# A gram product of 128 rows split into two of 64 rows, in two PSUM banks, in a three-layer CIN on one core

## The chip, the core and the metric

One core of one Trainium2 chip. The metric is the device time of one execution in microseconds (us); of several runs the median is taken. A difference of under 0.2% is about what a measurement of this kernel can't tell from no change.

## What is computed

A compressed interaction network over 512 samples, 39 fields of 16 dimensions each, three layers of 128 outputs, and a small dense tower behind it:

```python
def _cin_layer(X0, Xi, W, b):
    H = W.shape[0]
    F0_, Fi = (X0.shape[1], Xi.shape[1])
    Wr = W.reshape(H, F0_, Fi)
    return jnp.einsum('hjk,bjd,bkd->bhd', Wr, X0, Xi) + b[None, :, None]
X0 = embedded_features                 # 512 x 39 x 16, gathered from 39 tables
Xi = X0
for W, b in Ws:                        # 3 layers
    Xi = _cin_layer(X0, Xi, W, b)
    res.append(Xi.sum(axis=2))
h = concat(res, dense_ctx); y = relu(relu(h @ W_top1 + b1) @ W_top2 + b2) @ W_top3
```

Only the sum over the 16 dimensions of the third layer is wanted. So the kernel forms, for each sample, the product of the second layer's output with X0 summed over the dimensions (the *gram*: 128 outputs by 39 fields and one column of plain sums), and multiplies by the third layer's weights once at the end.

## The kernel before, in words

The batch is cut into 16 groups of 32 samples (`GROUPS`), each of 4 tiles (`TILES`) of 8 samples. A tile has 8 samples times 16 dimensions, so 128 rows, one per partition; rows 0 to 63 belong to its first four samples. T counts the 64 tiles through all groups, t is the tile in its group.

Each engine runs its own program and they meet through semaphores. In a tile the following is done:

- **TensorE** (PE) makes the second layer in ten *banks*, `layer1_bank` (L1111): bank m holds four fields (bank 9 three) times 128 outputs, by three products (L1124, L1125, L1128) of high and low halves. Before a bank it waits until the PSUM bank that it writes is free (`bank_free`, L1104). Banks 1, 2, 4, 5, 7, 8 and 9 go through a ring of four PSUM banks, banks 0, 3 and 6 through a ring of two. After bank 3 (`GRAM_AT`) stands the gram of the tile two back (`gram_product(T - 2, t % 2)`, L1096, its matmul L1101): the 128 rows of `x2` against `bdiag`, 8 samples times 40 columns, 320 columns into one PSUM bank, `pq`. It waits for `x2_ready`, `bdiag_ready` and the copy of the gram before. At seven slots of a group (`LAYER0_SLOTS`), one of them after bank 4 of tile 0, a piece of the next group's first layer stands (L1089 and, for two pieces, L1076 to L1086).
- **ScalarE** (ACT) scales the seven banks field by field, in place (L765). After bank 4 of tile 3 it also takes the next group's first layer out of PSUM (`high_part`, L733); after bank 4 of each tile it copies the gram two back from `pq` to SBUF (L737).
- **VectorE** (DVE) scales banks 0 and 3 into an accumulator of 9 columns per output (L914, counted by `dve_scaled`) and bank 6 in place (L919), adds the other banks to the accumulator (L935), and folds the accumulator into `x2` (L941), which sets `x2_ready`. In `low_part` (L896) it makes the low half of the next group's input.
- **GpSimd** (POOL) writes `bdiag` (`spread`, L544) for the tile: X0 times a mask, so that a row meets only its own sample's 40 columns. It waits for the gram of the tile two back, which read the same buffer. It also gathers the embeddings by indirect DMA (L497) and makes the first layer's pairs (L568).

The order on DVE is written out by hand. "sum before" and "fold before" belong to the tile in front:

```python
DVE_ORDER = (("sum before", 8), ("scale", 0), ("sum before", 9), ("scale", 3), ("sum", 1), ("sum", 2),
             ("sum", 4), ("fold before", 0), ("scale", 6), ("sum", 5), ("sum", 7), ("sum", 6))
SEAM_ORDER = tuple(x for x in DVE_ORDER if x[0] != "fold before") + (("fold before", 0),)
```

`SEAM_ORDER` holds for tile 3 of a group: the low half goes behind "sum 4" and the fold of tile 2 to the very end. The gram that reads this fold stands after bank 3 of tile 0 of the next group. There are 15 such seams. The groups 2 to 13 run in a loop of two, the others are written out. The program and its semaphores are otherwise the same in all tiles.

Of the kernel before, what the change touches and what calls it, by code (L numbers as in the profile page):

```python
# [5 lines left out]
F32 = mybir.dt.float32  # L6
F32R = mybir.dt.float32r
I32 = mybir.dt.int32
ALU = mybir.AluOpType
# [3 lines left out]
P = 128  # L13
BATCH, FIELDS, DIM, HID = 512, 39, 16, 128
# [5 lines left out]
TILE_B = P // DIM  # L20
# [4 lines left out]
NT = GROUPS * TILES  # L25
# [17 lines left out]
BANKS = -(-FIELDS // BANK_F)  # L43
LAST_F = FIELDS - BANK_F * (BANKS - 1)
GRAM = FIELDS + 1

ACT_BANKS = (1, 2, 4, 5, 7, 8, 9)  # L50
DVE_BANKS = (0, 3, 6)
N_ACT, N_DVE = len(ACT_BANKS), len(DVE_BANKS)
ACT_RING, DVE_RING = 4, 2
RING = ACT_RING + DVE_RING
N_ACC = 2
BEGINS = DVE_BANKS[0:N_ACC]
PARTS = N_ACC * BANK_F + 1


DVE_ORDER = (("sum before", 8), ("scale", 0), ("sum before", 9), ("scale", 3), ("sum", 1), ("sum", 2),  # L60
             ("sum", 4), ("fold before", 0), ("scale", 6), ("sum", 5), ("sum", 7), ("sum", 6))
SEAM_ORDER = tuple(x for x in DVE_ORDER if x[0] != "fold before") + (("fold before", 0),)
SUM_ORDER = (1, 2, 4, 5, 7, 6, 8, 9)
# [55 lines left out]
def tower(nc, dense_ctx, ids, table, bases, W_top1, b_top1, W_top2, b_top2, W_top3,  # L119
          W0, b0, W1, b1, W2, b2, out):  # L120
    ctx = ExitStack()
    with ctx:
        def sb(name, shape, dt=F32):
            return ctx.enter_context(nc.sbuf_tensor(name, shape, dt))

        def pb(name):
            return ctx.enter_context(nc.psum_tensor(name, [P, 512], F32))

        def sem(name):
            return ctx.enter_context(nc.semaphore(name))  # L130


        ident = sb("ident", [P, P])
        mask = sb("mask", [P, TILE_B])
        ids_all = sb("ids_all", [P, GROUPS, PER_Q], I32)
        base = sb("base", [P, PER_Q], I32)
        idx = [sb(f"idx{u}", [P, PER_Q], I32) for u in range(2)]
# [3 lines left out]
        x0t = [sb(f"x0t{u}", [P, TILES, COLS]) for u in range(2)]  # L141
# [10 lines left out]
        b1c = sb("b1c", [P, HID])  # L152
        acc = [sb(f"acc{u}", [P, HID, PARTS]) for u in range(2)]
        x2 = [sb(f"x2_{u}", [P, HID]) for u in range(2)]
        bdiag = [sb(f"bdiag{u}", [P, TILE_B, GRAM]) for u in range(2)]
        spare = [sb(f"spare{i}", [P, BATCH], F32R) for i in range(8)]
        ctx_wide = sb("ctx_wide", [P, TOP1], F32R)
        ctx_tall = sb("ctx_tall", [P, BATCH], F32R)
        gram = sb("gram", [P, GRAM, BATCH])
        z0 = sb("z0", [P, BATCH])  # L160
# [43 lines left out]
        x0d = nc.dram_tensor("x0_scratch", [2, ROWS_D, GROUP_N], F32, kind="Internal").ap()  # L204


        yb = [pb(f"yb{i}") for i in range(RING)]
        ya, yd = yb[0:ACT_RING], yb[ACT_RING:RING]
        p0 = pb("p0")
        pq = pb("pq")  # L210


        ids_in = sem("ids_in")
# [15 lines left out]
        consts = sem("consts")  # L229
# [28 lines left out]
        dve_scaled = sem("dve_scaled")  # L258
# [3 lines left out]
        gram_done = sem("gram_done")  # L262
        gram_copied = sem("gram_copied")
# [27 lines left out]
        def y_bank(t, m):  # L291

            if m in ACT_BANKS:
                return ya[(t * N_ACT + ACT_BANKS.index(m)) % ACT_RING]
            return yd[(t * N_DVE + DVE_BANKS.index(m)) % DVE_RING]

        def sums_by(T, m):

# [14 lines left out]
        def at_least(T, n):  # L313

            return not isinstance(T, int) or T >= n
# [41 lines left out]
        def _(sp):  # L357
# [101 lines left out]
            load_rolled(1, 1)  # L459
            period(0, 0)  # L460
            stack_weights()
            sp.wait_ge(consts, 10)
            for at in CTX_AT:
                sp.dma_start(dctx[:, :, at:at + CTX], dense_ctx.rearrange("(c p) n -> p c n", p=P)).then_inc(ctx_in, 16)
            period(1, 1)
# [18 lines left out]
        def _(pool):  # L484
# [10 lines left out]
            def gather(u, i):  # L495
# [3 lines left out]


            pool.memset(ident[:, :], 1.0).then_inc(consts, 1)
            pool.memset(mask[:, :], 1.0).then_inc(consts, 1)
            pool.wait_ge(consts, 1)
            pool.affine_select(out=ident[:, :], in_=ident[:, :], compare_op=ALU.is_equal, fill=0.0,
                               base=0, pattern=[[-1, P]], channel_multiplier=1).then_inc(consts, 1)
            pool.wait_ge(consts, 3)
            pool.affine_select(out=mask[:, :], in_=mask[:, :], compare_op=ALU.is_ge, fill=0.0,
                               base=0, pattern=[[-DIM, TILE_B]], channel_multiplier=1).then_inc(consts, 1)
            pool.wait_ge(consts, 4)
            pool.affine_select(out=mask[:, :], in_=mask[:, :], compare_op=ALU.is_ge, fill=0.0,  # L510
                               base=DIM - 1, pattern=[[DIM, TILE_B]], channel_multiplier=-1).then_inc(consts, 1)
            pool.wait_ge(consts, 5)
            for u in range(2):
                pool.tensor_copy(bdiag[u][:, :, FIELDS], mask[:, :]).then_inc(consts, 1)
            for u in range(2):
                pool.memset(emb[u][:, :, :], 0.0).then_inc(consts, 1)
            pool.memset(dctx[:, :, :], 0.0).then_inc(consts, 1)
            pool.wait_ge(consts, 9)
            pool.wait_ge(ids_in, 16 * 2)
            for u in range(2):  # L520
                if u == 1:
# [15 lines left out]
            def spread(g, t, u):  # L537
                T = g * TILES + t

                if t == 0:  # L540
                    pool.wait_ge(x0t_in[u], (g + 2 - u) * (8 * TILES))
                if at_least(T, 2):
                    pool.wait_ge(gram_done, T - 1)
                pool.tensor_tensor(bdiag[t % 2][:, :, 0:FIELDS],  # L544
                                   mask[:, :, None].to_broadcast([P, TILE_B, FIELDS]),
                                   x0t[u][:, t, None, 0:FIELDS].to_broadcast([P, TILE_B, FIELDS]),
                                   ALU.mult).then_inc(bdiag_ready, 1)

            def sum_dims(g, u):
# [122 lines left out]
        def _(act):  # L672
# [7 lines left out]
            def copy_weights(n):  # L680

                act.wait_ge(w_turned, n + 1)
                if n < W0_BANKS:
                    for i in range(4 * n, min(4 * n + 4, CHUNKS)):
                        rows = ROWS if i < CHUNKS - 1 else LAST_ROWS
                        op = act.activation(w0t[0:rows, i, :], yb[n % RING][0:rows, (i % 4) * HID:(i % 4 + 1) * HID], ACT.Copy)
                    op.then_inc(w_hi, 1)
                else:
                    j = 4 * (n - W0_BANKS)
                    w = min(4, FIELDS - j) * HID  # L690
                    act.activation(w1h[:, j * HID:j * HID + w], yb[n % RING][:, 0:w], ACT.Copy).then_inc(w_hi, 1)

# [42 lines left out]
            def copy_gram(T):  # L735
                act.wait_ge(gram_done, T + 1)
                act.activation(gram[:, :, bass.ds(T * TILE_B, TILE_B)],  # L737
                               pq[:, 0:TILE_B * GRAM].rearrange("p (b c) -> p c b", c=GRAM),
                               ACT.Copy).then_inc(gram_copied, 1)

            def high_weights():
# [123 lines left out]
        def _(dve):  # L865
# [17 lines left out]
            def low_weights(n):  # L883
# [3 lines left out]
                if n >= W0_BANKS + W_BANKS:  # L887
                    dve.tensor_copy(w2flat[:, j * HID:j * HID + w], yb[n % RING][:, 0:w]).then_inc(w_lo, 1)
                    return
                dve.wait_ge(w_hi, n + 1)  # L890
                dve.tensor_tensor(w1l[:, j * HID:j * HID + w], yb[n % RING][:, 0:w],
                                  w1h[:, j * HID:j * HID + w].bitcast(F32), ALU.subtract).then_inc(w_lo, 1)
# [103 lines left out]

        @block.tensor
        def _(pe):
            pe.wait_ge(consts, 9)
            pe.wait_ge(w0_sym, 2 * HALF + 1)  # L1000

            def wait_bank(n):
# [90 lines left out]
                if c == CHUNKS - 1:  # L1093
                    op.then_inc(l0_done, 1)

            def gram_product(T, p):  # L1096
                pe.wait_ge(x2_ready, T + 1)
                pe.wait_ge(bdiag_ready, T + 1)
                if at_least(T, 1):
                    pe.wait_ge(gram_copied, T)  # L1100
                pe.matmul(pq[:, 0:TILE_B * GRAM], x2[p][:, :], bdiag[p][:, :, :].rearrange("p b c -> p (b c)"),  # L1101
                          start=True, stop=True).then_inc(gram_done, 1)

            def bank_free(T, m):  # L1104

                if m in BEGINS:
                    pe.wait_ge(dve_scaled, T * N_DVE + BEGINS.index(m) + 1)
                else:
                    pe.wait_ge(summed, sums_by(T, m))

            def layer1_bank(g, t, u, m, low=None):  # L1111
                T = g * TILES + t
                of, ring = (ACT_BANKS, ACT_RING) if m in ACT_BANKS else (DVE_BANKS, DVE_RING)
                k = of.index(m)
                if k >= ring:
                    bank_free(T, of[k - ring])
                elif at_least(T, 1):
                    bank_free(T - 1, of[k - ring])
                y = y_bank(t, m)
                w = fields_of(m) * HID  # L1120
                at = BANK_F * m * HID
                cols = slice(t * P, (t + 1) * P)
                hi, lo = x1h[u][:, cols], x1l[u][:, cols]
                pe.matmul(y[:, 0:w], hi, w1h[:, at:at + w], start=True, stop=False)  # L1124
                pe.matmul(y[:, 0:w], hi, w1l[:, at:at + w], start=False, stop=False)  # L1125
                if low is not None:
                    pe.wait_ge(x1l_ready, low)
                pe.matmul(y[:, 0:w], lo, w1h[:, at:at + w], start=False,  # L1128
                          stop=True).then_inc(bank_ready, 1)
# [42 lines left out]
                period(it * 2 + 1, 1, 2)  # L1172
            period(GROUPS - 2, 0, 1)
            period(GROUPS - 1, 1, 0)
            gram_product(NT - 2, 0)

            def layer2_plain(h):

# [18 lines left out]
            pe.wait_ge(dense_split, 8)  # L1197
            pe.wait_ge(summed, NT * N_SUM)
            first_terms(0)
            gram_product(NT - 1, 1)  # L1200
            for c in range(1, TOP1 // P):
                first_terms(c)
            pe.wait_ge(gram_copied, NT)
# [1 line left out]
            for i in range(FIELDS - PLAIN):  # L1205
# [8 lines left out]
                op = pe.matmul(p0[:, :], w2h[:, w], gram_l[r], start=False, stop=(j == FIELDS - 1))  # L1214
# [16 lines left out]
            for c in range(TOP1 // P):  # L1231
                pe.matmul(yb[c][:, :], wt1h[2][:, c * P:(c + 1) * P], zl[2], start=False,
                          stop=True).then_inc(h1_done, 1)
            for c in range(TOP1 // P):
                pe.wait_ge(h1_ready, c + 1)
                for o in range(TOP2 // P):
                    op = pe.matmul(yd[o][:, :], wt2[:, c, o * P:(o + 1) * P], h1[c],  # L1237
                                   start=(c == 0), stop=(c == TOP1 // P - 1))
                    if c == TOP1 // P - 1:
                        op.then_inc(h2_done, 1)  # L1240
            for c in range(TOP2 // P):
                pe.wait_ge(h2_ready, c + 1)
                op = pe.matmul(p0[0:1, :], wt3[:, c:c + 1], h2[c], start=(c == 0), stop=(c == TOP2 // P - 1))
# [39 lines left out]
```

## Time and profile before

| what | value |
|---|---|
| median of 3 runs | 657.04 us |
| lowest and highest run | 656.72 and 657.56 us |
| span of the profiled execution, first to last instruction | 664.5 us |
| TensorE clock granted, mean over the span | 0.995 of full (1.0 is 2.4 GHz) |
| PE, DVE, ACT, POOL busy, share of the span | 95%, 85%, 84%, 67% |

The profiled execution is one of its own, and its span is the only time that the page gives of it. Its span is 7.5 us over the median of the runs that were timed without a profile. Times in rows are counted from its first instruction. The ends of matmuls are modelled: a matmul's row is longer than its share of the array, and the distance from the start of one to the start of the next tells what it costs. "x2" with the gram is its two weight loads and two passes, which the trace shows as two matmuls.

### The profile page before, as it was taken

How to read it: one execution, taken by the hardware profiler on the slowest of the kernel's cores; microseconds unless marked ns; L12 is line 12 of the kernel's file. 1: busy time of each engine (PE TensorE's matmuls, PEld its weight loads, DVE VectorE, ACT ScalarE, POOL GpSimd, SP SyncE). 2: the span in 40 equal slices, each digit the busy share in tenths (PEclk: the TensorE clock that was granted, in tenths of full speed). 3: DMA queues.
4: the chain of work that ended last, by engine and by line, in shares of the span. 5: the costliest groups of instructions: out<-in, count | busy, mean ns of one | idle time of the engine just before them, and what ended most of it. 6: DMA issues, size and time to landing. Idle time of an engine off the chain costs nothing.

```text
span 664.5 us, 11375 instructions
## 1 busy us (share of the span) xinstructions
PE 633.7 (95%) x2616; PEld 477.0 (72%) x2616; DVE 561.9 (85%) x878; ACT 557.3 (84%) x1940; POOL 443.1 (67%) x504
## 2 busy tenths in 40 slices
PE   2689999999999999999999999999999999989998
PEld 2656767777777777777777777777777777767874
DVE  3538788889899898989898989898989989899890
ACT  2348788989898999999998999998989998999773
POOL 7555897777777778687777787777777535152700
PEclk9799999999999999999999999999999999999999
DMA  8245533242424233242423333323242320200000
GB/s 292 22 61 105 162 38 87 51 87 56 84 56 80 59 58 84 40 102 33 90 41 84 57 86 55 87 52 81 57 85 55 67 68 6 69 27 0 1 0 1
DMA packets 91117, 43.58 MB, mean 66 GB/s; under 512 B 80630, under 2 KB 83780, under 8 KB 88943
## 3 DMA queue, kind: packets, MB, share of 16 engines
q1 hardware_dynamic: 84058, 41.77, 28.1%
q0 software_dynamic: 5120, 1.29, 2.2%
q10 hardware_dynamic: 1904, 0.15, 0.2%
q14 instruction: 25, 0.20, 0.1%
q8 instruction: 10, 0.16, 0.1%
HBM read 36.39 MB, written 1.81 MB: 57 GB/s over the span
## 4 chain that ended last, share of the span: by engine, by line
PE 75%; DVE 8%; ACT 7%; issue 6%; DMA 3%; DVEq 1%; POOL 0%; SPq 0%; another core or an unknown queue 0%
PE yb L1128 16%; PE yb L1124 16%; PE yb L1125 16%; PE p L1089 10%; PE pq L1101 6%; ACT yb L765 5%; DVE x L941 3%; DVE acc L935 3%; DMA gram<-in_L_rec_W_dram 2%; PE yb L1026 2%; DMA emb<-in_table_dram,idx 1%; DVE x1l L896 1%; PE yb L1237 1%; PE p L1182 1%; PE p L1214 1%
## 5 line engine op out<-in xcount | busy, mean ns | idle before, releaser
L765 ACT ACTIVATE yb<-yb,x0t 128x128 f32<-128x128 f32 x1728 | 467.2, 391 | 56.0 <-PE yb L1128 49.6
L935 DVE TENSOR_TENSOR acc<-acc,yb 128x512 f32<-128x512 f32 (+1 forms) x512 | 323.4, 674 | 33.8 <-ACT yb L765 30.9
L1124 PE MATMUL yb<-w1h,x1h 128*128 128x512 f32 (+1 forms) x640 | 293.8, 459 | 5.0 <-DVE acc L935 3.8
L1128 PE MATMUL yb<-w1h,x1l 128*128 128x512 f32 (+1 forms) x640 | 247.4, 387 | 0.0
L1125 PE MATMUL yb<-w1l,x1h 128*128 128x512 f32 (+1 forms) x640 | 247.1, 386 | 0.0
L497 POOL DMA_INDIRECT emb<-in_table_dram,idx x160 | 153.0, 956 | 53.1 <-issue 44.4
L1124 PEld LDWEIGHTS yb<-w1h,x1h 128*128 128x128 f32 x640 | 120.1, 188 | 59.4 <-DVE acc L935 25.3
L1125 PEld LDWEIGHTS yb<-w1l,x1h 128*128 128x128 f32 x640 | 120.5, 188 | 39.6 <-issue 18.0
L1128 PEld LDWEIGHTS yb<-w1h,x1l 128*128 128x128 f32 x640 | 120.1, 188 | 24.8 <-DVE x1l L896 0.4
L568 POOL TENSOR_TENSOR late<-late,x0r 117x512 f32<-117x512 f32 (+1 forms) x105 | 132.7, 1298 | 4.6 <-DMA late<-x_scratch 4.3
L544 POOL TENSOR_TENSOR bdiag<-mask,x0t 128x312 f32<-128x312 f32 x64 | 45.7, 714 | 107.0 <-PE pq L1101 106.4
L914 DVE TENSOR_TENSOR acc<-yb,x0t 128x512 f32<-128x512 f32 x128 | 88.7, 693 | 22.2 <-PE yb L1128 17.9
L1089 PE MATMUL p<-late,w0t 117*128 117x512 f32 (+1 forms) x168 | 86.1, 593 | 1.2 <-DVE late L970 0.9
L941 DVE TENSOR_REDUCE x<-acc 128x128 f32<-128x1152 f32 x64 | 86.5, 1351 | 0.1
L1101 PE MATMUL pq<-bdiag,x 128*128 128x320 f32 x128 | 46.4, 444 | 2.8 <-DVE x L941 2.8
L919 DVE TENSOR_TENSOR yb<-yb,x0t 128x512 f32<-128x512 f32 x64 | 44.5, 695 | 0.0
L591 POOL TENSOR_TENSOR spare<-late,spare 117x512 fp32r<-117x512 f32 (+1 forms) x28 | 35.6, 1298 | 4.9 <-ACT spare L754 4.6
L1089 PEld LDWEIGHTS p<-late,w0t 117*128 117x128 f32 (+1 forms) x168 | 31.0, 189 | 7.9 <-DVE late L970 1.7
L1101 PEld LDWEIGHTS pq<-bdiag,x 128*128 128x128 f32 x128 | 22.8, 188 | 13.2 <-issue 7.9
L737 ACT ACTIVATE gram<-pq 128x320 f32<-128x320 f32 x64 | 29.5, 462 | 1.2 <-PE pq L1101 1.2
L558 POOL TENSOR_TENSOR x1s<-x1s 128x256 f32<-128x256 f32 (+2 forms) x48 | 23.8, 496 | 3.8
L553 POOL TENSOR_TENSOR x1s<-x1h,x1l 128x512 f32<-128x512 f32 x16 | 20.5, 1281 | 0.0
(124 smaller groups left out, 377.2 us busy)
## 6 DMA issues: line engine op xcount, KB each, us to landing
late<-x_scratch SPq DMA_DIRECT2D x45, 312.0 KB
late<-x_scratch SPq DMA_DIRECT2D x30, 234.0 KB
x0r<-x_scratch SPq DMA_DIRECT2D x15, 234.0 KB
emb<-in_table_dram,idx POOLq DMA_INDIRECT x160
gram<-in_L_rec_W_dram SPq DMA_DIRECT2D x1, 2496.0 KB
late<-x_scratch SPq DMA_DIRECT2D x15, 156.0 KB
spare<-spare SPq DMA_DIRECT2D x28, 78.0 KB
x_scratch<-emb SPq DMA_DIRECT2D x75, 20.0 KB
```

The costliest lines, as they stand in the source:

```text
L497: pool.indirect_dma_start(emb[u][0:n, i, :], None, table[:, :], bass.IndirectOffsetOnAxis(idx[u][0:n, i:i + 1], 0)).then_inc(gathered[u], 16)
L544: pool.tensor_tensor(bdiag[t % 2][:, :, 0:FIELDS], mask[:, :, None].to_broadcast([P, TILE_B, FIELDS]), x0t[u][:, t, None, 0:FIELDS].to_bro ...
L568: pool.tensor_tensor(pairs[0:rows, c, :], pairs[0:rows, c, :], x0r[0:rows, :], ALU.mult).then_inc(pairs_ready, 1)
L765: op = act.activation(part, part, ACT.Copy, scale=x0t[u][:, t, j:j + 1])
L914: dve.tensor_tensor(acc[t % 2][:, :, at:at + BANK_F], parts(y, BANK_F), x0t[u][:, t, None, BANK_F * m:BANK_F * (m + 1)].to_broadcast([P, H ...
L935: dve.tensor_tensor(part, part, parts(y_bank(t, m), n), ALU.add).then_inc(summed, 1)
L941: dve.tensor_reduce(x2[t % 2][:, :], acc[t % 2][:, :, :], AX.X, ALU.add).then_inc(x2_ready, 1)
L1089: op = pe.matmul(p0[:, :], w0t[0:rows, c, :], pairs[0:rows, c, :], start=(c == 0), stop=(c == CHUNKS - 1))
L1101: pe.matmul(pq[:, 0:TILE_B * GRAM], x2[p][:, :], bdiag[p][:, :, :].rearrange("p b c -> p (b c)"), start=True, stop=True).then_inc(gram_don ...
L1124: pe.matmul(y[:, 0:w], hi, w1h[:, at:at + w], start=True, stop=False)
L1125: pe.matmul(y[:, 0:w], hi, w1l[:, at:at + w], start=False, stop=False)
L1128: pe.matmul(y[:, 0:w], lo, w1h[:, at:at + w], start=False, stop=True).then_inc(bank_ready, 1)
```

## The change

The 128 rows of the gram are two halves of 64 rows, each of four samples. Each half is a product of its own, 64 rows by 160 columns, and the two write to different PSUM banks: the first to the last 160 columns of the bank that also takes bank 0 of each tile, the second to the first 160 columns of what was `pq`. The two banks are neighbours, so ACT's copy still reads 320 columns in one. `bdiag` has 4 times 40 columns in place of 8 times 40, and `spread` writes 156 elements per row in place of 312.

Since the first half lands in bank 0's PSUM bank, the gram of T - 2 waits until DVE has scaled bank 0 of T, and bank 0 of the next tile waits for the copy of that gram. Banks 3 and 6 share the other PSUM bank: bank 6 waits for the scaling of bank 3 of its tile where it waited for bank 0. On DVE "scale 0" goes ahead of "sum before 8", in tile 3's order too. The mask gets one more small operation on POOL at the start.

```diff
-DVE_ORDER = (("sum before", 8), ("scale", 0), ("sum before", 9), ("scale", 3), ("sum", 1), ("sum", 2),
+DVE_ORDER = (("scale", 0), ("sum before", 8), ("sum before", 9), ("scale", 3), ("sum", 1), ("sum", 2),
              ("sum", 4), ("fold before", 0), ("scale", 6), ("sum", 5), ("sum", 7), ("sum", 6))
...
+YD_OF = (0, 1, 1)
...
-        bdiag = [sb(f"bdiag{u}", [P, TILE_B, GRAM]) for u in range(2)]
+        bdiag = [sb(f"bdiag{u}", [P, HALF_B, GRAM]) for u in range(2)]
...
+        two = pb("two", 2)
+        pq = two[:, 512:1024]
+        yb = [pb(f"yb{i}") for i in range(ACT_RING)] + [two[:, 0:512], pb("yd1")]
...
+        gram_out = two[:, 512 - HALF_GRAM:512 + HALF_GRAM]
...
+            pool.tensor_tensor(mask[:, :], mask8[:, 0:HALF_B], mask8[:, HALF_B:TILE_B], ALU.add).then_inc(consts, 1)
+            pool.wait_ge(consts, 6)
...
                 pool.tensor_tensor(bdiag[t % 2][:, :, 0:FIELDS],
-                                   mask[:, :, None].to_broadcast([P, TILE_B, FIELDS]),
-                                   x0t[u][:, t, None, 0:FIELDS].to_broadcast([P, TILE_B, FIELDS]),
+                                   mask[:, :, None].to_broadcast([P, HALF_B, FIELDS]),
+                                   x0t[u][:, t, None, 0:FIELDS].to_broadcast([P, HALF_B, FIELDS]),
                                    ALU.mult).then_inc(bdiag_ready, 1)
...
                 act.activation(gram[:, :, bass.ds(T * TILE_B, TILE_B)],
-                               pq[:, 0:TILE_B * GRAM].rearrange("p (b c) -> p c b", c=GRAM),
+                               gram_out.rearrange("p (b c) -> p c b", c=GRAM),
                                ACT.Copy).then_inc(gram_copied, 1)
...
-                pe.matmul(pq[:, 0:TILE_B * GRAM], x2[p][:, :], bdiag[p][:, :, :].rearrange("p b c -> p (b c)"),
-                          start=True, stop=True).then_inc(gram_done, 1)
+                pe.wait_ge(dve_scaled, (T + 2 if own is None else own) * N_DVE + 1)
+                for h in range(2):
+                    rows = slice(h * HALF_P, (h + 1) * HALF_P)
+                    op = pe.matmul(gram_out[:, h * HALF_GRAM:(h + 1) * HALF_GRAM], x2[p][rows, :],
+                                   bdiag[p][rows, :, :].rearrange("p b c -> p (b c)"), start=True, stop=True)
+                op.then_inc(gram_done, 1)
...
+                if m == DVE_BANKS[0]:
+                    if at_least(T, 3):
+                        pe.wait_ge(gram_copied, T - 2)
+                    elif at_least(T, 1):
+                        bank_free(T - 1, m)
+                elif m == DVE_BANKS[1]:
+                    if at_least(T, 1):
+                        bank_free(T - 1, DVE_BANKS[2])
+                elif m == DVE_BANKS[2]:
+                    bank_free(T, DVE_BANKS[1])
```

## Rows read from the trace of the kernel before

**Rows 1.** The page: busy time by engine; the chain that ended last, by line

```profile
PE 633.7 (95%) x2616; PEld 477.0 (72%) x2616; DVE 561.9 (85%) x878; ACT 557.3 (84%) x1940; POOL 443.1 (67%) x504
...
PE yb L1128 16%; PE yb L1124 16%; PE yb L1125 16%; PE p L1089 10%; PE pq L1101 6%; ACT yb L765 5%; DVE x L941 3%; DVE acc L935 3%; DMA gram<-in_L_rec_W_dram 2%; PE yb L1026 2%; DMA emb<-in_table_dram,idx 1%; DVE x1l L896 1%; PE yb L1237 1%; PE p L1182 1%; PE p L1214 1%
```

**Rows 2.** The chain of waits over one group (start us, us, what)

```profile
299.98 1.36 DVE x L941
...
301.46 0.80 PE pq L1101 x2
...
310.67 0.54 PE pq L1101 x2
...
330.07 0.86 ACT yb L765 x3
...
336.64 0.80 PE pq L1101 x2
```

**Rows 3.** Windows, the group from seam gram to seam gram: busy us (instructions) per engine

```profile
301.46:336.64 35.18, 35.01 (x143) 26.50 (x144) 32.08 (x50) 32.06 (x118) 26.99 (x30) 1.00 0.33 67
```

**Rows 4.** Line L1101: its matmuls, and what ended idle time before it

```profile
L1101 PE MATMUL pq<-bdiag,x x128: 430/431/537, 67.2 to 618.9; 128*128 128x320 f32 x128
  DVE x L941: 4.4, 17
```

**Rows 5.** Timeline, PE in tile 1, where nothing makes the gram wait

```profile
310.28 0.39 PE L1128 MATMUL yb<-w1h,x1l 128*128 128x512 f32 x1
310.51 0.70 PE L1101 MATMUL pq<-bdiag,x 128*128 128x320 f32 x2
...
311.29 0.40 PE L1125 MATMUL yb<-w1l,x1h 128*128 128x512 f32 x1
```

**Rows 6.** Timeline, DVE at the seam

```profile
301.24 0.68 DVE L935 TENSOR_TENSOR acc<-acc,yb 128x512 f32<-128x512 f32 x1
301.83 0.69 DVE L914 TENSOR_TENSOR acc<-yb,x0t 128x512 f32<-128x512 f32 x1
302.43 0.60 DVE L935 TENSOR_TENSOR acc<-acc,yb 128x384 f32<-128x384 f32 x1
```

**Rows 7.** Timeline, PE and its weight loads (PEld) at the seam

```profile
301.46 0.80 PE L1101 MATMUL pq<-bdiag,x 128*128 128x320 f32 x2 [0.18 <-DVE x L941]
...
302.32 0.39 PE L1125 MATMUL yb<-w1l,x1h 128*128 128x512 f32 x1
...
301.98 0.19 PEld L1124 LDWEIGHTS yb<-w1h,x1h 128*128 128x128 f32 x1 [0.23 <-DVE acc L935]
```

**Rows 8.** Timeline, tile 3, all engines; the first row is from tile 1

```profile
310.71 0.69 DVE L914 TENSOR_TENSOR acc<-yb,x0t 128x512 f32<-128x512 f32 x1
...
327.73 0.92 POOL L497 DMA_INDIRECT emb<-in_table_dram,idx  x1 [0.31 <-issue]
328.08 0.39 PE L1128 MATMUL yb<-w1h,x1l 128*128 128x512 f32 x1
329.72 0.69 DVE L914 TENSOR_TENSOR acc<-yb,x0t 128x512 f32<-128x512 f32 x1 [0.93 <-PE yb L1128]
...
331.71 6.07 ACT L765 ACTIVATE yb<-yb,x0t 128x128 f32<-128x128 f32 x23
333.37 1.88 DVE L935 TENSOR_TENSOR acc<-acc,yb 128x512 f32<-128x512 f32 x3
```

**Rows 9.** Groups by line and shape, POOL (count, busy us, mean ns, idle before)

```profile
L544 POOL TENSOR_TENSOR bdiag<-mask,x0t 128x312 f32<-128x312 f32 x64 | 45.7, 714 | 107.0 <-PE pq L1101 106.4
...
L558 POOL TENSOR_TENSOR x1s<-x1s 128x256 f32<-128x256 f32 x16 | 11.7, 733 | 1.3
L558 POOL TENSOR_TENSOR x1s<-x1s 128x128 f32<-128x128 f32 x16 | 7.3, 459 | 1.3
```

**Rows 10.** Timeline at the start, POOL

```profile
1.44 0.19 POOL L507 TENSOR_SCALAR_AFFINE_SELECT mask<-mask 128x8 f32<-128x8 f32 x1
1.71 0.19 POOL L510 TENSOR_SCALAR_AFFINE_SELECT mask<-mask 128x8 f32<-128x8 f32 x1
```

More of the change, by code:

```diff
@@ L45 @@
 GRAM = FIELDS + 1
+HALF_B = TILE_B // 2
+HALF_P = P // 2
+HALF_GRAM = HALF_B * GRAM
 ACT_BANKS = (1, 2, 4, 5, 7, 8, 9)
@@ L124, in sb, with pb @@
             return ctx.enter_context(nc.sbuf_tensor(name, shape, dt))
-        def pb(name):
-            return ctx.enter_context(nc.psum_tensor(name, [P, 512], F32))
+        def pb(name, banks=1):
+            return ctx.enter_context(nc.psum_tensor(name, [P, 512 * banks], F32))
         def sem(name):
@@ L133, in tower @@
         ident = sb("ident", [P, P])
-        mask = sb("mask", [P, TILE_B])
+        mask8 = sb("mask8", [P, TILE_B])
+        mask = sb("mask", [P, HALF_B])
         ids_all = sb("ids_all", [P, GROUPS, PER_Q], I32)
@@ L204, in tower @@
         x0d = nc.dram_tensor("x0_scratch", [2, ROWS_D, GROUP_N], F32, kind="Internal").ap()
-        yb = [pb(f"yb{i}") for i in range(RING)]
+        two = pb("two", 2)
+        pq = two[:, 512:1024]
+        yb = [pb(f"yb{i}") for i in range(ACT_RING)] + [two[:, 0:512], pb("yd1")]
         ya, yd = yb[0:ACT_RING], yb[ACT_RING:RING]
         p0 = pb("p0")
-        pq = pb("pq")
+        gram_out = two[:, 512 - HALF_GRAM:512 + HALF_GRAM]
         ids_in = sem("ids_in")
@@ L294, in y_bank @@
                 return ya[(t * N_ACT + ACT_BANKS.index(m)) % ACT_RING]
-            return yd[(t * N_DVE + DVE_BANKS.index(m)) % DVE_RING]
+            return yd[YD_OF[DVE_BANKS.index(m)]]
         def sums_by(T, m):
@@ L461, in _ @@
             stack_weights()
-            sp.wait_ge(consts, 10)
+            sp.wait_ge(consts, 11)
             for at in CTX_AT:
@@ L501, in _ @@
             pool.memset(ident[:, :], 1.0).then_inc(consts, 1)
-            pool.memset(mask[:, :], 1.0).then_inc(consts, 1)
+            pool.memset(mask8[:, :], 1.0).then_inc(consts, 1)
             pool.wait_ge(consts, 1)
@@ L506, in _ @@
             pool.wait_ge(consts, 3)
-            pool.affine_select(out=mask[:, :], in_=mask[:, :], compare_op=ALU.is_ge, fill=0.0,
+            pool.affine_select(out=mask8[:, :], in_=mask8[:, :], compare_op=ALU.is_ge, fill=0.0,
                                base=0, pattern=[[-DIM, TILE_B]], channel_multiplier=1).then_inc(consts, 1)
             pool.wait_ge(consts, 4)
-            pool.affine_select(out=mask[:, :], in_=mask[:, :], compare_op=ALU.is_ge, fill=0.0,
+            pool.affine_select(out=mask8[:, :], in_=mask8[:, :], compare_op=ALU.is_ge, fill=0.0,
                                base=DIM - 1, pattern=[[DIM, TILE_B]], channel_multiplier=-1).then_inc(consts, 1)
             pool.wait_ge(consts, 5)
+            pool.tensor_tensor(mask[:, :], mask8[:, 0:HALF_B], mask8[:, HALF_B:TILE_B], ALU.add).then_inc(consts, 1)
+            pool.wait_ge(consts, 6)
             for u in range(2):
@@ L517, in _ @@
             pool.memset(dctx[:, :, :], 0.0).then_inc(consts, 1)
-            pool.wait_ge(consts, 9)
+            pool.wait_ge(consts, 10)
             pool.wait_ge(ids_in, 16 * 2)
@@ L998, in _ @@
         def _(pe):
-            pe.wait_ge(consts, 9)
+            pe.wait_ge(consts, 10)
             pe.wait_ge(w0_sym, 2 * HALF + 1)
@@ L1094, in layer0, with gram_product @@
                     op.then_inc(l0_done, 1)
-            def gram_product(T, p):
+            def gram_product(T, p, own=None):
                 pe.wait_ge(x2_ready, T + 1)
@@ L1112, in layer1_bank @@
                 T = g * TILES + t
[L1113 to L1118, printed above, removed]
+                if m == DVE_BANKS[0]:
[8 more added lines that the diff above has]
+                    bank_free(T, DVE_BANKS[1])
+                else:
+                    k = ACT_BANKS.index(m)
+                    if k >= ACT_RING:
+                        bank_free(T, ACT_BANKS[k - ACT_RING])
+                    elif at_least(T, 1):
+                        bank_free(T - 1, ACT_BANKS[k - ACT_RING])
                 y = y_bank(t, m)
@@ L1174, in _ @@
             period(GROUPS - 1, 1, 0)
-            gram_product(NT - 2, 0)
+            gram_product(NT - 2, 0, NT - 1)
             def layer2_plain(h):
@@ L1199, in _ @@
             first_terms(0)
-            gram_product(NT - 1, 1)
+            gram_product(NT - 1, 1, NT - 1)
             for c in range(1, TOP1 // P):
```

## The prediction, made before the changed kernel was built or run

> **What bounds the kernel now.** I read the page first. PE is busy for 95% of the span, and the second layer's three product lines, the first layer's line and the gram make up most of the chain that ended last, the gram 6% of it [rows 1]. So a shorter gram can pay, if nothing else takes its place.
>
> The chain over one group shows where PE isn't the bound. It runs on PE from the gram of tile 0 (301.46) through tile 1's gram at 310.67, a gram there being 0.54 us of chain, to bank 4 of tile 3. There it goes over to ACT (330.07) and DVE, and comes back to PE when the fold lets the next group's first gram start at 336.64 [rows 2]. That is a period of 35.18 us. In it PE is busy for 35.01 us (its rows are modelled and overlong), DVE and ACT for about 32.1 us each, POOL for 27.0 us [rows 3]. The line of the gram says the same: 17 times it was a fold (L941) that let it go [rows 4]. There are 15 seams, so a group's gain or loss counts 15 times, and 64 - 17 = 47 grams wait for no fold.
>
> **The gram itself.** In tile 1, from the start of the last product in front (310.28) to the start of the second one behind (311.29) is 1.01 us; two products' pitch of 0.23 taken off leaves 0.55, the chain's 0.54 [rows 2, 5]. The change doesn't alter what is streamed in all: one product of 320 columns becomes two of 160, each in two passes. No row of before has a product of 64 rows or fewer, so the price of the pair must be bounded. Below: both halves entirely side by side, half of 0.54, a gain of 0.27. Between: the four passes go in order, and only the second pass of the first half stands beside the first pass of the second, three quarters of 0.54, a gain of 0.135. Above: the array empties ahead of the pair and behind it. A row of a product is 0.39 long at a pitch of 0.23, so 0.16 is what the array needs to empty [rows 5]. At the seam, where the gram starts on an empty array with its weights not yet loaded, it costs 302.32 - 0.23 - 301.46 = 0.63 in place of 0.54, so the weights are 0.09 [rows 7]. An emptying therefore costs 0.09 to 0.25, the two of them 0.18 to 0.50 per gram. I take 0, the same 0.54: the nearest row is the gram's own, and the columns are the same in sum.
>
> **DVE's order at the seam.** This is the part that I can price. Now the fold starts at 299.98 and is 1.36 long, and the gram starts at 301.46 [rows 2]. Behind the fold DVE has sum 8 (301.24), scale 0 (301.83) and sum 9 (302.43), at a pitch of 0.59 to 0.60 [rows 6]. In the changed order scale 0 follows the fold, and the first gram waits for it: 0.60 later, at about 302.06. Sum 8 then ends 0.60 later too, and bank 4's weights wait for just that sum already: the load at 301.98 was released by L935 [rows 7]. So even if the gram is shorter there, bank 4 of tile 0 starts 0.60 later. Sum 9 and all behind it keep their time. The chain ran through the fold and the gram, so nothing covers this: 15 x 0.60 = **+9.0 us**.
>
> **Shorter work on POOL.** spread falls from 312 to 156 elements. Two shapes of another POOL line differ by 733 - 459 = 274 ns for 128 elements, 2.1 ns each, so it gets 0.33 shorter, from 0.71 [rows 9]. POOL itself has idle time. But in tile 3 DVE starts scale 3 at 329.72, though bank 3's last product ends at 328.08 + 0.39 = 328.47; in tile 1 DVE starts at 310.71, 0.04 behind the product's end (310.28 + 0.39) [rows 5, 8]. A gather stands at 327.73 in the late case. That the late release follows the gathers is inferred, not shown. If it does, the spreads of tiles 1 and 2 bring it up to 0.67 forward. Little of that reaches the fold, because ACT ends the scaling of bank 7 after 8 of 23 pieces, 331.71 + 8/23 x 6.07 = 333.82, and sum 7 starts at 333.37 + 0.60 = 333.97: some 0.11 with the handover. That gives 0 to -15 x 0.11 = -1.7 us, and I take **-1.7 us**, since the gathers stand behind both spreads.
>
> **The rest, at nothing.** Bank 6 waits for scale 3 where it waited for scale 0. It is tightest in tile 3: scale 3 ends at 329.72 + 0.69 = 330.41; bank 6 would start at 328.31 + 0.54 + 8 pitches of 0.23 = 330.69 (banks 4 and 5 and two products of the first layer), its weights one pitch ahead at 330.46 [rows 8]. That holds by 0.05, and an earlier scale 3 widens it; a gram shorter by more would wait here unless scale 3 comes earlier too. Scale 0 ahead of sum 8 can make DVE wait for bank 0 in tiles 1 to 3; its 3.1 us of idle time in a group cover that [rows 3]. ACT copies 320 columns as before, from two banks. Behind POOL's wait for the gram, later at the seam, stand its gathers and pairs; its 8.2 us of idle time cover them [rows 3]. The operation more at the start is some 0.27, a pitch of its neighbours [rows 10], and the load of the weights, 2% of the span on the chain, hides it [rows 1]; without that cover it costs 0.3 once. No DMA is added or moved; SP's only new wait is a higher count of the same start.
>
> The **sum** is +9.0 - 1.7 = +7.3 us. Against the profiled span of 664.5 us that is 671.8 us. The span is 7.5 us above the median of the runs without a profile, so I carry the difference, not the ratio: 657.0 + 7.3 = **664.3 us**, 1.1% slower. A bound of the sum without POOL's part is 666.0.
>
> **Rivals.**
>
> *Half side by side.* The passes go in order and two of the four share the array. Then 47 x 0.135 = 6.3 us come off, 657.9 us, as good as no change. For it speaks that the halves use different rows and different banks; against it that no row shows two products in the array at once.
>
> *Wholly side by side.* 47 x 0.27 = 12.7 us come off, **651.6 us**, faster. This is the case on the other side: its place is the gram of tiles 1, 2 and 3, where PE alone makes the chain, and it decides from 7.3/47 = 0.155 us per gram on. DVE and ACT at 32.1 us of a period of 34.9 leave room. Against it: each half has two passes with two weight loads on the same rows, which have to follow one another.
>
> *The array empties on both sides.* Each gram of the 47 pays 0.18 to 0.50, less the 0.135 of passes that share the array: 0.05 to 0.37, or 2 to 17 us; the 15 at the seams pay behind the gram alone, 0.09 to 0.25, 1 to 4 us. The middle is 664.3 + 10 + 2.5 = **676.8 us**. For it: a product behind a wait does pay for its weights at the seam [rows 7]. Against it: products of 117 and of 128 rows follow each other now without a gap, but both fill more than half of the array.
>
> The Trainium skill bears on these three: TensorEngine Tiling (Array Packing), section Tiling Modes, says that tiles of the array work independently and can run in parallel, and that a change of the tiling mode drains TensorE. No run shown here has such a change. By the first rule alone the sum would be one of the two smaller figures, by both the last one.
>
> That the change doesn't do what it says, the two products simply following one another, is the forecast itself.
>
> **How the numbers follow.** About 0.34 for the forecast, 0.20 for half side by side, 0.14 for wholly, 0.32 for emptying. A measurement of this kernel can tell some 0.2%, 1.3 us, from no change. Faster takes all of wholly and the better part of half side by side where POOL's relief is larger, 0.20. Same is the rest of the latter, 0.14. Slower is 0.66. The range runs from just under wholly side by side, 651, to the middle of emptying and a bit over, 678; the dearer half of emptying is left out. The cases that are slower have a range of their own of 660 to 685.
>
> **What would show it.** Right: at the seam DVE shows fold, scale 0, sum 8, and the gram starts 0.6 behind the fold's end rather than 0.1; a period near 35.7 us; in tile 1 still 1.01 us between the product in front of the gram and the second one behind. There the rivals part: 0.88 and 0.74 us for half and wholly side by side, 1.06 to 1.4 us for emptying, with weight loads of the gram that start only behind the last product. Spread should take about 0.38. Wrong: a gram at the seam that doesn't move, a scale 0 that is done ahead of the fold's end, or a new wait of PE for scale 3 ahead of bank 6.

## The result, and the profile after

The changed kernel takes 672.83 us (median of 4 runs, 672.39 to 673.13), the kernel before beside it 657.30 us. The ratio is 1.0238, with a 95% interval of 1.0224 to 1.0253: 15.5 us slower. I had forecast 7.3 us slower, with a range of 651 to 678. The sign and the range held; the size was under half of what came.

The profiled span grew by less, from 664.5 to 671.4 us, because the first profile of the kernel before lost time in its start. The same kernel profiled again (the first run below) has a span of 654.5 us and reaches its first seam gram at 78.65 us in place of 85.33. In the first profile the granted clock stood at its lower level (0.50, 1.2 GHz) for 6.8 us of the start, from 24.4 us on; in the second it was 1.00 (2.4 GHz) throughout. That explains a part at most: at half the clock 6.8 us lose 3.4, and PE was already 2.9 us late before the clock fell (the first product with `w2t` started at 23.73 in place of 20.81 us, after waits of 1.57, 0.78 and 0.90 us for DVE). What held up that start is open. All comparisons here are therefore made with the second profile, and by the period from seam to seam, in which the clock was 1.00 in both kernels (the changed kernel's own profile has 3.4 us at the lower level, in its start).

From the page of the changed kernel: the busy times, and the chain by line.

```profile
PE 634.7 (95%) x2744; PEld 468.8 (70%) x2744; DVE 568.7 (85%) x878; ACT 559.1 (83%) x1940; POOL 426.4 (64%) x505
...
PE yb L1148 14%; PE yb L1152 12%; PE yb L1149 12%; PE p L1098 10%; ACT yb L774 5%; PE two L1114 4%; PE yd L1148 3%; PE yd L1149 3%; PE yd L1152 3%; DVE x L950 3%; DVE acc L944 3%; POOL emb L504 3%; DMA emb<-in_table_dram,idx 2%; PE two L1148 2%; PE two L1149 2%
```

No engine has become the bound; PE has the same share as before [rows 1]. (Lines have moved: the gram is L1114, a bank's products L1148, L1149 and L1152, scale 0 and 3 L923, the sums L944, the fold L950, spread L553.)

The windows of one period, from seam gram to seam gram: first the changed kernel, then the kernel before in its second profile. The columns are the length, then busy us of PE, its weight loads, DVE, ACT and POOL.

```profile
300.26:336.42 36.16, 35.20 (x151) 26.03 (x151) 32.66 (x50) 32.25 (x118) 25.95 (x30) 1.00 0.32 66
```

```profile
292.09:327.18 35.09, 34.83 (x144) 26.51 (x144) 32.40 (x50) 32.15 (x118) 26.93 (x30) 1.00 0.33 68
```

A period is 1.07 us longer, and 15 of them make 16.0 us, which is the measured difference but for 0.5. So nothing else of that size counts, and it is enough to find 1.07 us in a group.

**The seam.** The changed kernel's timeline there, all engines but POOL, as far as it bears on the gram:

```profile
334.30 1.34 DVE L950 TENSOR_REDUCE x<-acc 128x128 f32<-128x1152 f32 x1
335.68 0.69 DVE L923 TENSOR_TENSOR acc<-two,x0t 128x512 f32<-128x512 f32 x1
336.29 1.16 DVE L944 TENSOR_TENSOR acc<-acc,yb 128x512 f32<-128x512 f32 x2
...
336.42 0.54 PE L1114 MATMUL two<-bdiag,x 64*128 64x160 f32 x4 [0.92 <-DVE acc L923]
...
337.02 0.19 PEld L1148 LDWEIGHTS yb<-w1h,x1h 128*128 128x128 f32 x1 [0.29 <-DVE acc L944]
```

The kernel before, second profile, the same place:

```profile
325.70 1.34 DVE L941 TENSOR_REDUCE x<-acc 128x128 f32<-128x1152 f32 x1
326.96 0.68 DVE L935 TENSOR_TENSOR acc<-acc,yb 128x512 f32<-128x512 f32 x1
...
327.18 0.80 PE L1101 MATMUL pq<-bdiag,x 128*128 128x320 f32 x2 [0.26 <-DVE x L941]
...
327.69 0.19 PEld L1124 LDWEIGHTS yb<-w1h,x1h 128*128 128x128 f32 x1 [0.23 <-DVE acc L935]
```

The order is as forecast: fold, scale 0, sum 8, and the gram starts behind scale 0. Behind the start of the fold the gram starts after 336.42 - 334.30 = 2.12 us in place of 1.48, and bank 4's weights load after 2.72 in place of 1.99. That is 0.73 where I had 0.60. The missing 0.12 is in the second row: scale 0 starts 1.38 behind the start of the fold, while sum 8 in that place starts 1.26 behind it, before the fold's row has ended.

**The gram where nothing makes it wait.** The changed kernel, PE and its weight loads in tile 1 [rows 5]:

```profile
309.16 0.39 PE L1152 MATMUL yd<-w1h,x1l 128*128 128x512 f32 x1
309.48 0.54 PE L1114 MATMUL two<-bdiag,x 64*128 64x160 f32 x4
...
310.29 0.39 PE L1149 MATMUL yb<-w1l,x1h 128*128 128x512 f32 x1
...
309.48 0.30 PEld L1114 LDWEIGHTS two<-bdiag,x 64*128 64x128 f32 x4 [0.35 <-issue]
309.95 0.19 PEld L1148 LDWEIGHTS yb<-w1h,x1h 128*128 128x128 f32 x1 [0.17 <-issue]
```

From the product in front to the second one behind it is 1.13 us; two pitches of 0.23 off leave 0.67 in place of 0.55, so a gram is 0.125 us dearer, and within 0.01 us this holds in all 45 of the tiles 1 to 3 of groups 1 to 15 (two more grams, of group 0, lie in the start). The weight loads of the kernel before in the same place:

```profile
310.29 0.41 PEld L1101 LDWEIGHTS pq<-bdiag,x 128*128 128x128 f32 x2
...
310.78 0.19 PEld L1124 LDWEIGHTS yb<-w1h,x1h 128*128 128x128 f32 x1
```

There the gram's first load started with the product in front (310.28) and cost no time of its own. Now it starts at 309.48, 0.32 behind the start of that product, whose share of the time (0.23) is over at 309.39. Bank 4's load starts at 309.95, and its product streams from 310.29 - 0.23 = 310.06 on, so 0.11 us of this load are hidden by nothing. Bank 4's own waits are those of before, so no new semaphore holds it up. I read this as an array that empties twice; the trace shows the late loads, not the array.

So a period's 1.07 us are 0.73 at the seam and 0.34 in the three other tiles, where 3 x 0.125 = 0.375 came on. POOL's shorter spread (448 ns in place of 714 [rows 9]; I had said 380) brings back at most the 0.035 between them.

### The profile page after: what moved, and what is told of

It reads as the page before. It is cut to its first block, busy times and chain, and to the rows that moved or that the text cites. A ratio compares the mean times of both kernels' runs of the same rounds, so it can differ in the third digit from the quotient of the medians.

```text
span 671.4 us, 11644 instructions
## 1 busy us (share of the span) xinstructions
PE 634.7 (95%) x2744; PEld 468.8 (70%) x2744; DVE 568.7 (85%) x878; ACT 559.1 (83%) x1940; POOL 426.4 (64%) x505
## 4 chain that ended last, share of the span: by engine, by line
PE 76%; DVE 7%; ACT 7%; issue 4%; POOL 3%; DMA 2%; DVEq 1%; ACTq 0%; POOLq 0%
PE yb L1148 14%; PE yb L1152 12%; PE yb L1149 12%; PE p L1098 10%; ACT yb L774 5%; PE two L1114 4%; PE yd L1148 3%; PE yd L1149 3%; PE yd L1152 3%; DVE x L950 3%; DVE acc L944 3%; POOL emb L504 3%; DMA emb<-in_table_dram,idx 2%; PE two L1148 2%; PE two L1149 2%
## 5 line engine op out<-in xcount | busy, mean ns | idle before, releaser
L944 DVE TENSOR_TENSOR acc<-acc,yb 128x512 f32<-128x512 f32 (+1 forms) x448 | 283.4, 666 | 38.0 <-ACT yb L774 37.9
L1148 PE MATMUL yb<-w1h,x1h 128*128 128x512 f32 (+1 forms) x448 | 204.3, 456 | 4.0 <-DVE acc L944 3.2
L1152 PE MATMUL yb<-w1h,x1l 128*128 128x512 f32 (+1 forms) x448 | 172.2, 384 | 0.0
L1149 PE MATMUL yb<-w1l,x1h 128*128 128x512 f32 (+1 forms) x448 | 171.9, 384 | 0.0
L1148 PEld LDWEIGHTS yb<-w1h,x1h 128*128 128x128 f32 x448 | 84.0, 187 | 48.9 <-issue 19.2
L553 POOL TENSOR_TENSOR bdiag<-mask,x0t 128x156 f32<-128x156 f32 x64 | 28.7, 448 | 134.8 <-PE two L1114 134.3
L1149 PEld LDWEIGHTS yb<-w1l,x1h 128*128 128x128 f32 x448 | 84.4, 188 | 26.8 <-issue 14.4
L1152 PEld LDWEIGHTS yb<-w1h,x1l 128*128 128x128 f32 x448 | 84.1, 188 | 15.8
L950 DVE TENSOR_REDUCE x<-acc 128x128 f32<-128x1152 f32 x64 | 86.1, 1346 | 0.1
L923 DVE TENSOR_TENSOR acc<-yd,x0t 128x512 f32<-128x512 f32 x64 | 44.1, 689 | 14.5 <-PE yd L1152 14.5
L923 DVE TENSOR_TENSOR acc<-two,x0t 128x512 f32<-128x512 f32 x64 | 44.3, 691 | 9.1 <-PE two L1152 7.6
L1148 PE MATMUL yd<-w1h,x1h 128*128 128x512 f32 x128 | 50.8, 397 | 0.0
L1149 PE MATMUL yd<-w1l,x1h 128*128 128x512 f32 x128 | 49.9, 390 | 0.0
L1152 PE MATMUL yd<-w1h,x1l 128*128 128x512 f32 x128 | 49.9, 390 | 0.0
L1114 PE MATMUL two<-bdiag,x 64*128 64x160 f32 x256 | 34.7, 348 | 14.2 <-DVE acc L923 14.2
L1114 PEld LDWEIGHTS two<-bdiag,x 64*128 64x128 f32 x256 | 19.4, 184 | 37.9 <-issue 16.6
L928 DVE TENSOR_TENSOR yd<-yd,x0t 128x512 f32<-128x512 f32 x64 | 44.1, 689 | 0.0
L944 DVE TENSOR_TENSOR acc<-acc,yd 128x512 f32<-128x512 f32 x64 | 43.6, 681 | 0.0
```

Of the source, the lines that this page charges most:

```text
L923: dve.tensor_tensor(acc[t % 2][:, :, at:at + BANK_F], parts(y, BANK_F), x0t[u][:, t, None, BANK_F * m:BANK_F * (m + 1)].to_broadcast([P, H ...
L928: dve.tensor_tensor(y, y, x0t[u][:, t, BANK_F * m:BANK_F * (m + 1), None].to_broadcast([P, BANK_F, HID]), ALU.mult).then_inc(dve_scaled, 1)
L944: dve.tensor_tensor(part, part, parts(y_bank(t, m), n), ALU.add).then_inc(summed, 1)
L950: dve.tensor_reduce(x2[t % 2][:, :], acc[t % 2][:, :, :], AX.X, ALU.add).then_inc(x2_ready, 1)
L1114: op = pe.matmul(gram_out[:, h * HALF_GRAM:(h + 1) * HALF_GRAM], x2[p][rows, :], bdiag[p][rows, :, :].rearrange("p b c -> p (b c)"), start ...
L1152: pe.matmul(y[:, 0:w], lo, w1h[:, at:at + w], start=False, stop=True).then_inc(bank_ready, 1)
```

## The experiments

Theory A: the loss is scale 0 between the fold and sum 8 at the seam (with its wait for the fold), and the change to 64 rows and back in the other tiles. The theories B differ from run to run. Each run was compared with the kernel before on the same chip.

**The kernel before again.** No edit.

> The kernel before, unchanged, profiled once more. It settles whether the 7.2 us by which the first profiled span (664.5) lies over the median (657.3) belong to the kernel. Both theories: the period from seam gram to seam gram stays 35.18 us and a gram in tile 1 costs 0.545 us. Theory A (the first profile lost its time in the start, where the granted clock stood at half its speed for 6.8 us): the first seam gram starts near 80 us in place of 85.3, the span is near 656. Theory B (profiling stretches this kernel): the span is again near 664.

One run of 656.2 us, span 654.5, first seam gram at 78.65 us, period 35.09 (windows above). The 7.2 us weren't the kernel's, and profiling doesn't stretch it: theory B falls. Of theory A the time holds, and the cause, the lower clock, in part only, as said above. The period, too, was 0.09 shorter than in the first profile.

**The order alone**, in the kernel before:

```diff
-DVE_ORDER = (("sum before", 8), ("scale", 0), ("sum before", 9), ...
+DVE_ORDER = (("scale", 0), ("sum before", 8), ("sum before", 9), ...
```

> The kernel before with the changed order on DVE alone (scale 0 ahead of sum 8), its gram of 128 rows in one bank. Theory A (behind the fold scale 0 takes the place of sum 8, and bank 4 of tile 0 waits for sum 8): the gram at the seam still starts 1.48 us behind the start of the fold, but bank 4's weights load 2.7 us behind it in place of 2.0; 15 x 0.72 = 10.8 us slower, about 668 us. Theory B (the order costs nothing by itself, the time comes from the gram's new wait and from the two products): 657.3 us.

667.0 against 656.4 us, ratio 1.0161 (1.0144 to 1.0178): 10.6 us. DVE, then PE and its weight load at a seam of this kernel:

```profile
331.13 1.35 DVE L941 TENSOR_REDUCE x<-acc 128x128 f32<-128x1152 f32 x1
332.51 0.69 DVE L914 TENSOR_TENSOR acc<-yb,x0t 128x512 f32<-128x512 f32 x1
333.12 1.16 DVE L935 TENSOR_TENSOR acc<-acc,yb 128x512 f32<-128x512 f32 x2
...
332.61 0.80 PE L1101 MATMUL pq<-bdiag,x 128*128 128x320 f32 x2 [0.27 <-DVE x L941]
...
333.85 0.19 PEld L1124 LDWEIGHTS yb<-w1h,x1h 128*128 128x128 f32 x1 [0.95 <-DVE acc L935]
```

The gram starts 1.48 behind the start of the fold, as before, and gains nothing by it: bank 4's weights wait for sum 8 until 2.72 behind it, as in the changed kernel. The period is 35.81 us, so 0.72 of the 1.07 us. Two thirds of the loss are in one line of the diff, and the gram has no part in them. Theory B falls.

**The changed kernel with the old order:**

```diff
-DVE_ORDER = (("scale", 0), ("sum before", 8), ("sum before", 9), ...
+DVE_ORDER = (("sum before", 8), ("scale", 0), ("sum before", 9), ...
```

> The changed kernel with the old order on DVE (sum 8 ahead of scale 0). Theory A: the gram at the seam waits for sum 8 and scale 0, so it starts 2.6 us behind the start of the fold in place of 2.13, and bank 4 follows 0.47 us later at 3.07 in place of 2.72: 15 x 0.35 = 5.3 us more than the changed kernel, about 678 us. Theory B (the loss is the gram's own): as the changed kernel, 672.8 us.

678.38 against 656.39 us, ratio 1.0329 (1.0312 to 1.0346). DVE and PE at the seam:

```profile
336.56 1.34 DVE L950 TENSOR_REDUCE x<-acc 128x128 f32<-128x1152 f32 x1
337.82 0.68 DVE L944 TENSOR_TENSOR acc<-acc,yb 128x512 f32<-128x512 f32 x1
338.42 0.68 DVE L923 TENSOR_TENSOR acc<-two,x0t 128x512 f32<-128x512 f32 x1
...
339.16 0.54 PE L1114 MATMUL two<-bdiag,x 64*128 64x160 f32 x4 [1.39 <-DVE acc L923]
```

The gram starts 2.60 behind the start of the fold, and by the two ratios this costs 6.0 us more than the changed kernel, where 5.3 were expected. So the changed order is right for the changed kernel, in which the gram needs scale 0: it costs less than the other one, but the need for it is what costs.

**Two products of 128 rows**, in the kernel before; each takes four samples' columns, all rows, the same bank:

```diff
-                pe.matmul(pq[:, 0:TILE_B * GRAM], x2[p][:, :], bdiag[p][:, :, :]...
+                half = TILE_B // 2
+                for h in range(2):
+                    op = pe.matmul(pq[:, h * half * GRAM:(h + 1) * half * GRAM], x2[p][:, :],
+                                   bdiag[p][:, h * half:(h + 1) * half, :]...
```

> The kernel before with the gram as two products of 160 columns, each of all 128 rows, into the same bank. Theory A (the array empties because the tile of the array changes, from 128 rows to 64 and back): without that change two products cost what one did, a gram in tile 1 stays at 0.55 us, 657.3 us. Theory B (two products and four weight loads are dearer by themselves): 0.67 us as in the changed kernel, 47 x 0.125 = 5.9 us slower, 663.2 us.

656.56 against 656.39 us, ratio 1.0001 (0.9991 to 1.0011). PE in a tile without a wait:

```profile
320.03 0.39 PE L1132 MATMUL yb<-w1h,x1l 128*128 128x512 f32 x1
320.25 0.70 PE L1103 MATMUL pq<-bdiag,x 128*128 128x160 f32 x4
...
321.03 0.40 PE L1129 MATMUL yb<-w1l,x1h 128*128 128x512 f32 x1
```

1.00 us from the product in front to the second behind, so 0.54 for the gram, four passes of 0.135. Twice the products and weight loads cost nothing. What is left of the change in the changed kernel is the 64 rows and the second PSUM bank. A change of bank alone has no price: in the changed kernel's tile 1 the products go from `yb` (308.48) to `yd` (308.71) at the usual 0.23. So it is the 64 rows that cost.

**Both products on the same 64 rows**, in the changed kernel:

```diff
-                    rows = slice(h * HALF_P, (h + 1) * HALF_P)
+                    rows = slice(0, HALF_P)
```

> The changed kernel with both products of the gram on rows 0 to 63; the second four samples' rows are left out of the gram. Theory A (the two halves stand in the array at once only because their rows differ; their streaming is 0.27 us of the gram's 0.67, and 0.40 is emptying and loading): on the same rows they follow each other, a gram in tile 1 costs 0.67 + 0.27 = 0.94 us, three in a group, 45 x 0.27 = 12.2 us, and at the seam bank 4 comes 0.15 later, 2.3 us: about 687 us. Theory B (the halves don't share the array, the short time is that of 64 rows): as the changed kernel, 672.8 us.

688.1 against 657.1 us, ratio 1.0474 (1.0456 to 1.0491). PE in a tile without a wait:

```profile
333.56 0.39 PE L1152 MATMUL yd<-w1h,x1l 128*128 128x512 f32 x1
333.88 0.81 PE L1114 MATMUL two<-bdiag,x 64*128 64x160 f32 x4
...
334.95 0.40 PE L1149 MATMUL yb<-w1l,x1h 128*128 128x512 f32 x1
```

1.39 us, less two pitches 0.94: 0.27 more than on different rows. In the changed kernel, then, four passes of 0.135 take the time of two. Its halves do stand in the array wholly side by side, and what was saved so, 0.27, is less than the 0.67 - 0.27 = 0.40 paid for the change of the rows.

**The pair twice**, in the changed kernel:

```diff
-                for h in range(2):
+                for h in (0, 1, 0, 1):
```

> The changed kernel with the pair of products issued twice in a row, the second pair writing the same values again. Theory A (0.40 us of a gram in tile 1 are paid once, for the change to tiles of 64 rows and back; only the 0.27 of streaming are paid per pair): 0.67 + 0.27 = 0.94 us, as with both products on the same rows, about 688 us. Theory B (each product pays its own loading and emptying): 2 x 0.67 = 1.34 us, 45 x 0.67 + 15 x 0.5 = 38 us more, about 710 us.

688.26 against 657.08 us, ratio 1.0477 (1.0461 to 1.0493). PE in a tile without a wait:

```profile
333.06 0.39 PE L1152 MATMUL yd<-w1h,x1l 128*128 128x512 f32 x1
333.38 0.81 PE L1114 MATMUL two<-bdiag,x 64*128 64x160 f32 x8
...
334.46 0.40 PE L1149 MATMUL yb<-w1l,x1h 128*128 128x512 f32 x1
```

1.40 us, 0.94 for two grams' worth. The 0.40 are paid per change, not per product; a second pair, which goes through both banks again, costs 0.27.

**The first layer's piece ahead of the seam's wait.** In tile 0 the piece behind bank 4 goes behind bank 2, once in the changed kernel, once in the kernel before:

```diff
-LAYER0_SLOTS = ((0, 4), (0, 9), (1, 4), (1, 8), (2, 4), (2, 9), (3, 4))
+LAYER0_SLOTS = ((0, 2), (0, 9), (1, 4), (1, 8), (2, 4), (2, 9), (3, 4))
```

> The changed kernel with the first layer's piece of tile 0 behind bank 2 in place of bank 4. Theory A (at the seam PE waits 1.1 us for the fold and scale 0, and this wait is on the path): the 0.86 us of the piece move into the wait, 14 seams x 0.86 = 12.0 us off, 660.8 us, and the period falls from 36.16 to about 35.3. Theory B (another engine sets the period): less than 4 us off.

> The kernel before with the first layer's piece of tile 0 behind bank 2. Theory A: the wait at the seam is 0.44 us, so the piece fills it and the gram itself then starts later; 14 x 0.44 = 6.2 us off, 651.1 us. Theory B (another engine sets the period): no change, 657.3 us.

The changed kernel falls to 661.8 us beside 657.1 for the kernel before (ratio 1.0077, 1.0060 to 1.0093), 11.0 us less than the changed kernel with the piece in its old place, where 12.0 were expected (10.6 by the ratios); the period is 35.29. This is theory A: PE stood idle there. The windows of the changed kernel with this edit:

```profile
295.49:330.78 35.29, 35.17 (x152) 26.03 (x152) 32.46 (x50) 32.07 (x118) 25.98 (x30) 1.00 0.34 67
```

The kernel before came to 655.0 against 657.1 us (ratio 0.9971, 0.9957 to 0.9986): faster, but by a third of what was expected (its ten runs spread from 653.0 to 656.4). Its period did fall to 34.69. The rest was lost once, in group 1, where PE met the piece too soon. Its timeline:

```profile
81.10 1.10 PE L1089 MATMUL p<-late,w0t 117*128 117x512 f32 x2 [2.01 <-POOL late L568]
```

The first seam gram stood at 82.74 in place of 78.65. POOL starts on that pair at 79.67 in this run, behind eight gathers from 68.64 on. So group 1 got its old slot back, in the kernel before:

```diff
-                        slots = FIRST_LAYER0_SLOTS if first else LAYER0_SLOTS
+                        early = not (isinstance(g, int) and g == 1)
+                        slots = FIRST_LAYER0_SLOTS if first else (((0, 2),) if early else ((0, 4),)) + LAYER0_SLOTS[1:]
```

> The kernel before with the first layer's piece of tile 0 behind bank 2 from group 2 on; in group 1 it stays behind bank 4. Theory A (the early piece took 0.40 us off each period but waited 2 us and more in group 1, where POOL hadn't made the first pairs yet): the first seam gram is back near 78.6 us, the period stays 34.69, 13 x 0.40 = 5.2 us off, ratio 0.992, about 651.5 us. Theory B (the early piece costs in the start in another way): as before, ratio 0.997.

651.72 against 657.08 us, ratio 0.9926 (0.9913 to 0.9940): 5.4 us faster than the kernel before, and better than both kernels of the case. Its windows over one period:

```profile
290.00:324.69 34.69, 34.69 (x145) 26.51 (x144) 32.25 (x50) 32.06 (x118) 26.97 (x30) 1.00 0.35 68
```

By its rows, which are overlong, PE is now busy through the whole period.

**A third accumulator**, in the changed kernel:

```diff
-        acc = [sb(f"acc{u}", [P, HID, PARTS]) for u in range(2)]
+        acc3 = [sb(f"acc{u}", [P, HID, PARTS]) for u in range(3)]
+        acc = [acc3[0], acc3[1], acc3[2], acc3[1]]
...
-                    if m == BEGINS[0] and at_least(T, 2):
-                        dve.wait_ge(x2_ready, T - 1)
+                    back = 4 if t % 2 == 0 else 2
+                    if m == BEGINS[0] and at_least(T, back):
+                        dve.wait_ge(x2_ready, T - back + 1)
...
```

> The changed kernel with a third accumulator, so that tiles 0 and 2 of a group don't share one (two buffers of the start are moved into unused room of another). In the changed kernel scale 0 of tile 0 writes the accumulator that the fold in front of it reads, and waits for that fold's end. Theory A (that wait is 0.12 us of the seam's 0.72): scale 0 starts 1.26 us behind the start of the fold in place of 1.38, gram and bank 4 come 0.12 earlier, 15 x 0.12 = 1.8 us less than the changed kernel, ratio to the kernel before near 1.021 in place of 1.0238. Theory B (the 0.12 is the switch from one operation to the other on DVE, not a wait): 1.38 stays, ratio 1.0238.

670.31 against 657.08 us, ratio 1.0206 (1.0193 to 1.0220); that of the changed kernel was 1.0238: 2.1 us less, where 1.8 were expected. DVE at a seam:

```profile
332.42 1.34 DVE L952 TENSOR_REDUCE x<-acc 128x128 f32<-128x1152 f32 x1
333.68 0.68 DVE L925 TENSOR_TENSOR acc<-two,x0t 128x512 f32<-128x512 f32 x1
```

Scale 0 starts 1.26 behind the start of the fold, so the 0.12 was the wait for a fold that read the same accumulator. Sum 8, which adds to the other one, never had it.

## Why the prediction was right in sign and too small

- **The bound** was read rightly: PE through the group, DVE from the fold to the first gram, 15 times. The period's 1.07 us, 15 times, is the measured difference but for 0.5.
- **DVE's order at the seam**, "+9.0 us", was the right mechanism and a little small. The order alone measured 10.6 us. The term of 0.60 was 0.73, as scale 0 was priced by the pitch of sums that wait for nothing; the code's wait for `x2_ready` ahead of bank 0's scaling stood in the text that I read, and it became a wait for the operation just in front only through the move. That bank 4's weights hang on sum 8, so that the gram's own length doesn't count there, held.
- **The gram's price is the step that failed**: "I take 0, the same 0.54: the nearest row is the gram's own, and the columns are the same in sum." It is 0.67, and 45 x 0.125 = 5.6 us are most of what the forecast lacked. The lower and the upper bound were both paid at once: 0.27 less for halves that share the array, 0.40 more for emptying it twice and for weight loads that nothing hides, within the 0.18 to 0.50 that the rows gave. I had set these against each other as rivals where they are one case. The rival of emptying even added a part of the gain, but the half of it, because I held that the two passes of one half have to follow those of the other. Both passes of both halves run in pairs. That rival's own sign came: 1.13 us in tile 1, where it had 1.06 to 1.4, and weight loads that start only behind the last product. The range held because its upper end was drawn for this rival, not for the forecast.
- The Trainium skill, TensorEngine Tiling (Array Packing), section Tiling Modes, states both rules, that tiles can run in parallel and that a change of the tiling mode drains TensorE. This case's runs agree with both: 0.27 us saved by the first, and 0.40 us paid for the change there and back.
- **POOL's shorter spread**, "-1.7 us", gave 0.03 of a period at most, 0.5 us in all. The late start of scale 3 in tile 3 [rows 8], 0.93 us of idle time on which it rested, was 0.38 in the second profile of the same kernel: I had built a term on a wait that came and went with the execution. It is 0.27 in the changed kernel, and 0.27 with the order alone too, where spread is as long as before (712 ns), so what moved it is not the spread. Why it was longer in the first profile is open.
- **Nothing for the rest** held: no wait of PE for scale 3 ahead of bank 6, a copy of the same length from two banks (0.46 us), no engine newly short of time.

In the terms of the sum: 7.3, and 1.8 for the fold's wait, and 5.6 for the gram, and 1.2 for what POOL didn't bring, make 15.9 us; 15.5 were measured.

## What to carry to other kernels

A short product on part of the rows, alone between products on all rows, pays for two changes of the array: here 0.40 us for a saving of 0.27. It would have to stand in one place with others of its kind (two pairs together cost 0.94 us where two whole products, at 0.545 each, come to 1.09; grouping the grams of two tiles was not tried). When an operation is moved to stand directly behind another one, price it with its waits, not by the pitch that others have in that place. And a wait of the bounding engine that can't be shortened can be filled: the piece that was moved ahead of it took 5.4 us off the kernel before, while splitting the gram had cost 15.5.

## What the runs showed that was not expected

Two halves with two passes each, on different rows and different banks, take the array for the time of two passes, not of three: 0.67 against 0.94 us on the same rows. And the first profile of the kernel before was 10.0 us longer than the second (664.5 and 654.5), of which 6.7 lay ahead of the first seam, and of these the stretch at the lower clock explains 3.4 at most. One profiled span is a poor measure to set a sum against; the period from seam to seam differed by 0.09 us only.
